# Twelve late row tiles: 32x32 turns on VectorE and transfers through DRAM in place of TensorE transposes

## The chip, the cores and the metric

The kernel runs on one core of a Trainium2 chip. Its time is the device time of the run in microseconds (us).

## What is computed

`x` is 4 batches of 512 rows of 512. Four stages each add a gated term to it. The change is about the hand-over into the third stage.

```python
x = x + tanh(g_xattn[0]) * L0_xattn(layernorm(x), ctx, ...)   # attention with one head of 128
x = x + tanh(g_ffn[0])   * L0_ffn(layernorm(x), ...)          # 512x512 product with bit planes
x = x + tanh(g_xattn[1]) * L1_xattn(layernorm(x), ctx, ...)   # 16 heads of 128, rms-normalised q and k
x = x + tanh(g_ffn[1])   * L1_ffn(layernorm(x), ...)          # 16 experts, the first batch's rows
# L1_xattn:
q, k = rmsnorm(h @ Wq, gq), rmsnorm(ctx @ Wk, gk)             # per head
out = softmax(q @ k.T / sqrt(128)) @ (ctx @ Wv)
return out @ Wo
```

## The kernel before

Each product is made of three matmuls on float32 values split in a high part (`_hi`) and the rest (`_lo`), so every operand is written twice: ScalarE mostly writes the high part, VectorE or GpSimd the rest.

The third stage runs as 64 items, `ITEMS`: first the 16 heads of batch 0, then for each head the batches 1, 2 and 3. It is a pipeline of steps `t`: in step `t` item `t` gets its keys, values and queries, item `u = t - 1` its scores and softmax, and item `w = t - 2` its product with the values and with `Wo`. Every engine has its own program, written out by hand in the function `step(t)` of that engine. Each runs its instructions in order, and semaphores tie them together. A step therefore starts on the engines at different times. Below, "step 10" means the instructions of `step(10)` on whatever engine.

Of SyncE the queue of transfers matters. In step `t` it issues, in this order and each behind its own wait: the key and value weights of the next head (`stage<-w`, buffer 0), the store of the probability pair (`turn<-prob`), the four loads that bring it back turned (`prob<-turn`), the query weights of the next head (`stage<-w`, buffer 1), and the output weights (buffer 2). The pair is two of the four 128x512 probability tiles of item `t - 1`. VectorE turns its 32x32 blocks in place (line 1580, `turn_quads`), and the store and loads put the blocks where they belong.

ScalarE begins `step(t)` by writing the high part of the turned pair (`moved_hi`). Then it copies the output weights (`split_wo`) and the query weights (`split_wq`) to their high parts, then the first key and value rows (`first_rows`, line 1071), and then comes the first exponential of the scores (`softmax(0)`, line 1032). `turn_quads` on VectorE waits for the second one, `softmax(1)`.

The projections of batches 1 to 3 need the layer-normalised `x` with its columns in the partitions (`xnT`). These twelve 128x512 row tiles are the late tiles: `LATE` gives one each to the steps 4 to 15. Batch 1 is first used in step 16. A tile in step `t` before the change:

- ScalarE, first thing in the step: `late_norm` (line 1185) writes the normalised rows to `xn`.
- TensorE, between two parts of the key and value products: `late_turn` (line 817), four 128x128 transposes into the bank `w_bank[1]`. It waits for `late_norm` and for VectorE to have emptied the bank.
- ScalarE: `late_copy` writes `xnT_hi` from the bank, between `first_rows` and `softmax(0)`.
- VectorE: `late_lower` writes `xnT_lo`, behind the two shifts that release `softmax(0)` and `softmax(1)`.
- TensorE waits for `late_lo` ahead of the second output product, since that one reuses the bank.

In the steps 4 to 15 all of this is one tile in each step of one head.

## Time and profile before

| | us |
|---|---|
| Median of 3 runs | 1406.72 (1406.38 to 1410.99) |
| The profiled execution's own time | 1406.11 |
| Its span | 1404.3 |
| TensorE matmul busy | 1376.5 |
| VectorE busy | 1140.6 |
| ScalarE busy | 976.5 |
| GpSimd busy | 942.4 |

The span is the time from the first to the last instruction of the trace. Positions ("at 307.20") are us from its start. A step's length is read as the distance between the same instruction of two steps on one engine. The names in a row are those of the program, output first, with buffer numbers left out.

### The profile page before, as it was taken

Reading aid. Unit: us, or ns where it says so; the run is one execution under the profiler, and the core shown is the slowest. Engines: PE = TensorE matmul, PEld = TensorE weight load, DVE = VectorE, ACT = ScalarE, POOL = GpSimd, SP = SyncE. Lnnn points to the kernel's source line nnn. Section 1 sums busy time; section 2 is a strip of 40 time slices with the busy share of each in tenths; the row PEclk is TensorE's granted clock in tenths of the full one; section 3 lists DMA queues with packets and bytes.
Section 4 is the critical chain, followed back from the end, with each engine's and each line's share of the span. In section 5 each row is a group of like instructions: output and inputs, shape, how many; then the busy total and the mean of one; then the engine's idle time right before and its main releaser. Section 6 shows DMA issues by size and latency. Waiting matters only on the chain.

```text
span 1404.3 us, 23125 instructions
## 1 busy us (share of the span) xinstructions
PE 1376.5 (98%) x7614; PEld 1175.1 (84%) x7614; DVE 1140.6 (81%) x2072; ACT 976.5 (70%) x2165; POOL 942.4 (67%) x729
## 2 busy tenths in 40 slices
PE   8899999999999999999999999999999999999998
PEld 6778778888888888888888888888888888877886
DVE  7888778788888888887878888887878787888777
ACT  7863467788876767667676767667676766666764
POOL 4876557777776567667676767676776757776561
PEclk9999999999999999999999999999999999999999
DMA  9420023333433555656564646566565653442312
GB/s 338 156 78 16 23 75 107 106 117 116 122 113 113 167 167 183 190 168 193 176 200 156 204 160 189 183 179 188 174 198 163 189 170 125 138 145 94 98 61 90
DMA packets 135734, 204.59 MB, mean 146 GB/s; under 512 B 10112, under 2 KB 70528, under 8 KB 135616
## 3 DMA queue, kind: packets, MB, share of 16 engines
q1 hardware_dynamic: 131856, 190.79, 42.7%
q0 software_dynamic: 3760, 12.32, 3.3%
q8 instruction: 62, 1.02, 0.3%
q14 instruction: 56, 0.46, 0.1%
HBM read 157.72 MB, written 45.35 MB: 145 GB/s over the span
## 4 chain that ended last, share of the span: by engine, by line
PE 76%; DVE 3%; POOL 2%; ACT 2%; DMA 1%; issue 1%; SPq 0%; ACTq 0%; POOLq 0%
PE j_bank L578 9%; PE j_bank L580 9%; PE j_bank L579 9%; PE w_bank L578 8%; PE w_bank L580 8%; PE w_bank L579 8%; PE s_bank L578 4%; PE s_bank L580 3%; PE s_bank L579 3%; PE t_bank L655 3%; PE t_bank L613 2%; PE t_bank L578 1%; PE t_bank L579 1%; PE t_bank L580 1%; PE w_bank L761 1%
## 5 line engine op out<-in xcount | busy, mean ns | idle before, releaser
L1032 ACT ACTIVATE prob<-s_bank,neg_bias,q_scale 128x512 f32<-128x512 f32 x255 | 197.4, 777 | 141.5 <-DVE neg_bias L1545 141.5
L1613 DVE SCALAR_TENSOR_TENSOR x_sb<-w_bank,inv_sum,x_sb 128x512 f32<-128x512 f32 x254 | 186.7, 745 | 32.0 <-PE w_bank L580 30.9
L1947 POOL TENSOR_TENSOR xnT_lo<-xnT_raw,xnT_hi 128x512 fp32r<-128x512 f32 (+2 forms) x47 | 126.4, 2691 | 63.1 <-ACT xnT_hi L990 63.1
L1524 DVE TENSOR_REDUCE neg_max<-s_bank 128x1 f32<-128x512 f32 x255 | 168.0, 679 | 0.9 <-PE s_bank L580 0.9
L578 PE MATMUL j_bank<-wkv_lo,cT_hi 128*128 128x256 f32 x512 | 145.0, 283 | 0.0
L1947 POOL TENSOR_TENSOR cT_round<-cT_raw,x_round 128x1408 fp32r<-128x1408 f32 (+1 forms) x31 | 104.4, 3367 | 59.9 <-ACT x_round L990 59.9
L580 PE MATMUL j_bank<-wkv_hi,cT_lo 128*128 128x256 f32 x512 | 144.4, 282 | 0.0
L579 PE MATMUL j_bank<-wkv_hi,cT_hi 128*128 128x256 f32 x512 | 144.2, 282 | 0.0
L1988 POOL TENSOR_TENSOR q_scale<-q_ss,minus_half 128x4 f32<-128x4 f32 x64 | 66.0, 1031 | 106.3 <-DVE q_ss L1537 106.3
L1947 POOL TENSOR_TENSOR sqs_lo<-xn,sqs_hi 128x512 fp32r<-128x512 f32 x62 | 104.0, 1677 | 34.5 <-ACT xn L1120 33.8
L1580 DVE STREAM_TRANSPOSE prob<-prob 128x1024 f32<-128x1024 f32 x59 | 73.5, 1245 | 60.8 <-ACT prob L1032 60.4
L1385 DVE TENSOR_TENSOR probT_lo<-t_bank,probT_hi 128x512 fp32r<-128x512 f32 x142 | 97.5, 687 | 23.1 <-ACT probT_hi L990 22.9
L1947 POOL TENSOR_TENSOR kv_lo<-kv_raw,kv_hi 128x512 fp32r<-128x512 f32 x68 | 89.1, 1311 | 37.0 <-DVE kv_hi L1594 35.7
L578 PE MATMUL w_bank<-wo_lo,oT_hi 128*128 128x512 f32 x254 | 107.9, 425 | 1.2 <-issue 1.0
L578 PE MATMUL s_bank<-kv_lo,qT_hi 128*128 128x512 f32 x255 | 106.6, 418 | 1.0 <-ACT prob L1032 0.5
L578 PE MATMUL j_bank<-xnT_lo,wq_hi 128*128 128x512 f32 x256 | 106.0, 414 | 1.0 <-POOL wq_lo L1947 1.0
L579 PEld LDWEIGHTS j_bank<-wkv_hi,cT_hi 128*128 128x128 f32 x512 | 97.2, 190 | 5.5
L578 PEld LDWEIGHTS j_bank<-wkv_lo,cT_hi 128*128 128x128 f32 x512 | 97.2, 190 | 5.2
L580 PE MATMUL j_bank<-xnT_hi,wq_lo 128*128 128x512 f32 x256 | 100.5, 392 | 0.0
L580 PE MATMUL s_bank<-kv_hi,qT_lo 128*128 128x512 f32 x255 | 100.2, 393 | 0.0
L580 PE MATMUL w_bank<-wo_hi,oT_lo 128*128 128x512 f32 x254 | 100.1, 394 | 0.0
L579 PE MATMUL j_bank<-xnT_hi,wq_hi 128*128 128x512 f32 x256 | 99.9, 390 | 0.0
(312 smaller groups left out, 4600.2 us busy)
## 6 DMA issues: line engine op xcount, KB each, us to landing
turn<-prob SPq DMA_DIRECT2D x59, 512.0 KB, 3.1
prob<-turn SPq DMA_DIRECT2D x236, 128.0 KB, 3.2
stage<-w SPq DMA_DIRECT2D x96, 256.0 KB, 3.5
xnT_raw<-w_gu SPq DMA_DIRECT2D x31, 704.0 KB, 4.5
cT_raw<-w_gu SPq DMA_DIRECT2D x31, 704.0 KB, 5.9
xnT_raw<-w_dn SPq DMA_DIRECT2D x16, 768.0 KB, 5.4
cT_raw<-w_dn SPq DMA_DIRECT2D x15, 768.0 KB, 5.4
planes<-bits SPq DMA_DIRECT2D x16, 512.0 KB, 5.0
```

The source lines that it names most:

```text
L578: pe.matmul(dst, lh, rl, start=first, stop=False)
L579: pe.matmul(dst, lh, rh, start=False, stop=False)
L580: return pe.matmul(dst, ll, rh, start=False, stop=last)
L613: last = pe.transpose(t_bank[0][:, j * P:(j + 1) * P], kv_raw[:, j, 0:HD], ident[:])
L655: last = pe.transpose(prob_bank(t, i)[:, j * P:(j + 1) * P], prob[:, i, j * P:(j + 1) * P], ident[:])
L1032: nc.scalar.activation(dst, src, ACT.Exp, bias=neg_bias[:, u % 2, i:i + 1], scale=q_scale[:, u % 2, i:i + 1], accum_out=row_sum[:, u % 2, ...
L1385: return nc.vector.tensor_tensor(dst, src, hi, ALU.subtract)
L1524: nc.vector.tensor_reduce(neg_max[:, u % 2, i:i + 1], score_bank(t, i)[:], AX_X, ALU.max, negate=True).then_inc(own_max, 1)
L1580: nc.vector.transpose(flat_pair, flat_pair).then_inc(p_quads, 1)
L1613: nc.vector.scalar_tensor_tensor(out=here, in0=w_bank[0][:] if packed else out_bank(t, i)[:], scalar=inv_sum[:, w % 2, i:i + 1], in1=here, ...
L1947: return nc.gpsimd.tensor_tensor(dst, src, hi, ALU.subtract)
L1988: nc.gpsimd.tensor_tensor(q_scale[:, u % 2, :], q_ss[:, u % 2, :], minus_half[:], ALU.pow).then_inc(q_scale_ready, 1)
```

## The change

A late tile is no longer turned by TensorE. In step `t`:

- ScalarE writes the normalised rows with the columns reordered in groups of 32 (`late_blocks`). It does so between `late_copy` and `softmax(0)` and no longer first in the step.
- VectorE turns the 32x32 blocks of the tile in place (`late_turn`, 128x512), in the place where `late_lower` was.
- SyncE stores the tile to a third plane of `turn` ahead of the pair's store, and reads it back with four loads behind the pair's loads, ahead of the query and output weights.
- In step `t + 1` ScalarE writes `xnT_hi` from `xn` (`late_copy(t - 1)`, in the old place), and GpSimd writes `xnT_lo` (`late_lower(t - 1)`) ahead of `scale_keys`.
- TensorE has neither the four transposes nor the wait for `late_lo` ahead of the second output product. It waits for the tiles of a batch once, at that batch's first query product (`LATE_NEEDED`).

```diff
--- before.py
+++ after.py
@@ -91,6 +91,7 @@
 TURN, TURNS = numbered("DFPR", L0_ORDER)
 LATE = {4 + n: key for n, key in enumerate((b, i) for b in range(1, B) for i in range(NT))}
 LATE_HEAD = min(LATE)
+LATE_NEEDED = {next(t for t, item in enumerate(ITEMS) if item[1] == b): NT * b for b in range(1, B)}
 XN, XNS = numbered("df", ACT_ORDER)
 MOMENTS, NMOMENTS = numbered("mCE", DVE_ORDER)
 SHIFT = {key: n for n, key in enumerate(key for key in POOL_ORDER if key[0] in "CE")}
@@ -311,7 +312,11 @@
         def late_tile(part, t):
 
             b, i = LATE[t]
-            return xnT[part][:, b, :, i * P:(i + 1) * P]
+            return xnT[part][:, b, :, i * P:(i + 1) * P].rearrange("p j (r c) -> p j r c", c=QUAD)
+
+        def late_blocks(t):
+
+            return late_row(t).rearrange("p (r j c) -> p j r c", j=DT, c=QUAD)
 
         def late_row(t):
 
...
@@ -493,7 +499,25 @@
                 sp.wait_ge(p_stored, 16 * (MOVES[u] + 1))
                 for c in range(NT):
                     sp.dma_start(prob[c * QUAD:(c + 1) * QUAD, 0:2, :].rearrange("a i (r m) -> a (i r) m", r=NT),
-                                 turn_dram.rearrange("i (r a) (c m) -> c a (i r) m", r=NT, c=NT)[c]).then_inc(p_moved, 16)
+                                 turn_dram[0:2].rearrange("i (r a) (c m) -> c a (i r) m", r=NT, c=NT)[c]).then_inc(p_moved, 16)
+
+            def store_late(t):
+
+                if t not in LATE:
+                    return
+                n = t - LATE_HEAD
+                sp.wait_ge(late_turned, n + 1)
+                wait(sp, late_moved, 16 * NT * n)
+                sp.dma_start(turn_dram[2], late_row(t)).then_inc(late_stored, 16)
+
+            def load_late(t):
+
+                if t not in LATE:
+                    return
+                sp.wait_ge(late_stored, 16 * (t - LATE_HEAD + 1))
+                for c in range(NT):
+                    sp.dma_start(late_row(t)[c * QUAD:(c + 1) * QUAD, :].rearrange("a (r m) -> a r m", r=NT),
+                                 turn_dram[2].rearrange("(r a) (c m) -> c a r m", r=NT, c=NT)[c]).then_inc(late_moved, 16)
 
             def expert(b):
                 return sp.value_load(block_expert[0:1, b:b + 1], min_val=0, max_val=E - 1)
@@ -539,8 +563,10 @@
                 if fresh(t):
                     key_weights(SET[t] + 1)
                 if not in_block(t):
+                    store_late(t)
                     store_pair(t - 1)
                     load_pair(t - 1)
+                    load_late(t)
                 if fresh(t):
                     query_weights(SET[t] + 1)
                 if fresh(t - 2):
@@ -682,8 +708,6 @@
                         return
                     if t == LAST_VALUES and i == 2:
                         need(pe, o_lo, 1, w, 2)
-                    if t in LATE and i == 1:
-                        pe.wait_ge(late_lo, t - LATE_HEAD + 1)
                     if i == 0:
                         if not packed:
                             need(pe, o_lo, 1, w, 1)
@@ -727,6 +751,8 @@
                     if 0 in tiles:
                         if fresh(t):
                             pe.wait_ge(wq_lo, SET[t] + 1)
+                        if t in LATE_NEEDED:
+                            pe.wait_ge(late_lo, LATE_NEEDED[t])
                         need(pe, kv_first, 1, t, 1)
                     for dj in tiles:
                         last = product(j_bank[1][:], [a[:, dj * HD:(dj + 1) * HD] for a in wq],
@@ -807,15 +833,6 @@
                                 last = product(w_bank[0][:, to:to + width], here,
                                                [a[:, half, at:at + width] for a in (hi, lo)], j == 0, j == IT - 1)
                     last.then_inc(d_mm, 1)
-
-                def late_turn():
-                    if t not in LATE:
-                        return
-                    pe.wait_ge(late_normed, t - LATE_HEAD + 1)
-                    need(pe, w_added, 4, w, 0)
-                    for j in range(DT):
-                        last = pe.transpose(w_bank[1][:, j * P:(j + 1) * P], late_row(t)[:, j * P:(j + 1) * P], ident[:])
-                    last.then_inc(late_turned, 1)
 
                 def key_values():
                     key_value(0)
@@ -870,7 +887,6 @@
                     key_value(0, (0,))
                     query_squares()
                     key_value(0, (1,))
-                    late_turn()
                     key_value(1)
                     values()
                     if t == 2:
@@ -1181,15 +1197,16 @@
                     b, i = LATE[t]
                     act.wait_ge(shift_ready, SHIFT["E", b] + 1)
                     act.wait_ge(blocks_ready, 1)
-                    wait(act, late_turned, t - LATE_HEAD - 1)
-                    nc.scalar.activation(late_row(t), x_sb[:, b, i, :], ACT.Identity, bias=ln_shift[:, b, i:i + 1],
+                    wait(act, late_lo, t - LATE_HEAD - 1)
+                    row = x_sb[:, b, i, :].rearrange("p (j r c) -> p j r c", j=DT, c=QUAD)
+                    nc.scalar.activation(late_blocks(t), row, ACT.Identity, bias=ln_shift[:, b, i:i + 1],
                                          scale=rstd[:, b, i:i + 1]).then_inc(late_normed, 1)
 
-                def late_copy():
-                    if t not in LATE:
-                        return
-                    act.wait_ge(late_turned, t - LATE_HEAD + 1)
-                    copy_hi(late_tile(0, t), w_bank[1][:].rearrange("p (j q) -> p j q", j=4)).then_inc(late_hi, 1)
+                def late_copy(v):
+                    if v not in LATE:
+                        return
+                    act.wait_ge(late_moved, 16 * NT * (v - LATE_HEAD + 1))
+                    copy_hi(late_tile(0, v), late_blocks(v)).then_inc(late_hi, 1)
 
                 if t == 0:
                     return key_parts, query_parts, query_squares, key_hi
@@ -1229,7 +1246,6 @@
                     if t + 1 < NI and fresh(t + 1):
                         split_wkv(t + 1)
 
-                late_norm()
                 if not in_block(t - 1):
                     moved_hi(w)
                 if packed:
@@ -1265,7 +1281,8 @@
                 if fresh(t):
                     split_wq(t)
                 first_rows()
-                late_copy()
+                late_copy(t - 1)
+                late_norm()
                 softmax(0)
                 softmax(1)
                 second_rows()
@@ -1693,12 +1710,11 @@
                     need(dve, q_squared, 2, t, 2)
                     lower(sqs[1][:], squares(t), f32(sqs[0][:])).then_inc(sq_lo, 1)
 
-                def late_lower():
+                def late_turn():
                     if t not in LATE:
                         return
-                    dve.wait_ge(late_hi, t - LATE_HEAD + 1)
-                    lower(late_tile(1, t), w_bank[1][:].rearrange("p (j q) -> p j q", j=4),
-                          f32(late_tile(0, t))).then_inc(late_lo, 1)
+                    dve.wait_ge(late_normed, t - LATE_HEAD + 1)
+                    nc.vector.transpose(late_row(t), late_row(t)).then_inc(late_turned, 1)
 
                 def key_values_lo():
                     key_lo()
@@ -1799,7 +1815,7 @@
                     block_experts()
                 shift(0)
                 shift(1)
-                late_lower()
+                late_turn()
                 if t == T0 - 2:
                     dve.wait_ge(w_added, 4 * (LAST[0] + 1))
                     statistics(0, 0, NMOMENTS)
@@ -2054,6 +2070,12 @@
                     need(pool, q_squared, 2, t, 2)
                     lower(sqs[1][:], squares(t), f32(sqs[0][:])).then_inc(sq_lo, 1)
 
+                def late_lower(v):
+                    if v not in LATE:
+                        return
+                    pool.wait_ge(late_hi, v - LATE_HEAD + 1)
+                    lower(late_tile(1, v), late_blocks(v), f32(late_tile(0, v))).then_inc(late_lo, 1)
+
                 if t == 0:
                     return scale_keys, squares_lo, values_lo
                 if up:
@@ -2070,6 +2092,7 @@
                 if t > 2 and fresh(t):
                     lower_wq(t)
                 gate_up_lo()
+                late_lower(t - 1)
                 scale_keys()
                 take_y(2)
                 values_lo()
...
```

SyncE's queue in one step with a late tile, before. The names are tile and tensor, output first, and the waits are the semaphores on which the row waits. The three `stage<-w1` rows are the key and value weights (waits `wkv_lo`), the query weights (`wq_lo`) and the output weights (`wo_lo`):

```order
L466 DMA stage<-w1 128x512 [waits wkv_lo]
L487 DMA turn<-prob 128x2x512 [waits p_moved,p_quads]
L495 DMA prob<-turn 32x8x128 [waits p_stored]
L495 DMA prob<-turn 32x8x128 x3
L466 DMA stage<-w1 128x512 [waits wq_lo]
L466 DMA stage<-w1 128x512 [waits wo_lo]
```

The same place of the queue in the changed kernel:

```order
L472 DMA stage<-w1 128x512 [waits wkv_lo]
L511 DMA turn<-xn 128x512 [waits late_moved,late_turned]
L493 DMA turn<-prob 128x2x512 [waits p_moved,p_quads]
L501 DMA prob<-turn 32x8x128 [waits p_stored]
L501 DMA prob<-turn 32x8x128 x3
L519 DMA xn<-turn 32x4x128 [waits late_stored]
L519 DMA xn<-turn 32x4x128 x3
L472 DMA stage<-w1 128x512 [waits wq_lo]
L472 DMA stage<-w1 128x512 [waits wo_lo]
```

The tile's store stands ahead of the pair's store, and its four loads (32 partitions of four pieces of 128 elements each) stand between the pair's loads and the query and output weights.

ScalarE at the start of a step with a late tile, from the layer norm to the two exponentials that the pair's turn waits for, before (`xn<-x_sb` is `late_norm`, `xnT_hi` is `late_copy`):

```order
L1185 ACTIVATE xn<-x_sb,ln_shift,rstd 128x512 [waits late_turned,blocks_ready,shift_ready]
L990 CAST probT_hi<-prob 128x8x4x32 [waits pv_mm,p_moved]
L990 CAST wo_hi<-stage 128x512 [waits w_mm,wo_in]
L990 CAST wq_hi<-stage 128x512 [waits q_mm,wq_in]
L1071 COPY kv_raw<-j_bank1 128x512 [waits v_lo,kT_mm,kv_mm]
L990 CAST xnT_hi<-w_bank1 128x4x128 [waits late_turned]
L1032 ACTIVATE prob,row_sum<-s_bank0,neg_bias,q_scale 128x4x4x32 [waits pair_lo,s_max]
```

ScalarE at the same place in the changed kernel:

```order
L1006 CAST probT_hi<-prob 128x8x4x32 [waits pv_mm,p_moved]
L1006 CAST wo_hi<-stage 128x512 [waits w_mm,wo_in]
L1006 CAST wq_hi<-stage 128x512 [waits q_mm,wq_in]
L1087 COPY kv_raw<-j_bank1 128x512 [waits v_lo,kT_mm,kv_mm]
L1006 CAST xnT_hi<-xn 128x4x128 [waits late_moved]
L1202 ACTIVATE xn<-x_sb,ln_shift,rstd 128x4x4x32 [waits late_lo,blocks_ready,shift_ready]
L1048 ACTIVATE prob,row_sum<-s_bank0,neg_bias,q_scale 128x4x4x32 [waits pair_lo,s_max]
```

The layer norm moved from the front of the step to a place behind the weights' copies and `late_copy`, directly ahead of the two exponentials, and `late_copy` now waits for the transfers (`late_moved`).

## Rows read from the trace of the kernel before

**Rows 1.** The page's heading and its busy times, share of the span in brackets.

```profile
span 1404.3 us, 23125 instructions
PE 1376.5 (98%) x7614; PEld 1175.1 (84%) x7614; DVE 1140.6 (81%) x2072; ACT 976.5 (70%) x2165; POOL 942.4 (67%) x729
```

**Rows 2.** Busy time by stretch: twelve steps with a late tile, then two without.

```profile
core 0: us, PE busy (x) PEld busy (x) DVE busy (x) ACT busy (x) POOL busy (x), PEclk, DMA share, GB/s
205.00:392.00 187.00, 187.00 (x1050) 159.79 (x1049) 150.68 (x281) 150.17 (x355) 139.60 (x116) 1.00 0.38 116
404.00:435.00 31.00, 31.00 (x171) 26.27 (x170) 24.02 (x46) 22.35 (x56) 19.89 (x18) 1.00 0.30 95
```

**Rows 3.** Timeline (start us, us, engine, line): first matmul of the query squares, once a step.

```profile
210.13 0.39 PE L742 MATMUL t_bank<-sqs_hi,ones 128*128 128x512 f32 x1
226.28 0.39 PE L742 MATMUL t_bank<-sqs_hi,ones 128*128 128x512 f32 x1
...
403.84 0.40 PE L742 MATMUL t_bank<-sqs_hi,ones 128*128 128x512 f32 x1
419.54 0.39 PE L742 MATMUL t_bank<-sqs_hi,ones 128*128 128x512 f32 x1
435.24 0.39 PE L742 MATMUL t_bank<-sqs_hi,ones 128*128 128x512 f32 x1
```

**Rows 4.** Line 817, all TensorE turns of the late tiles: ns min/median/max, first and last start.

```profile
L817 PE MATMUL w_bank<-ident,xn x48: 270/272/276, 211.3 to 389.2; 128*128 128x128 f32 x48
```

**Rows 5.** Timeline of SyncE's queue: pair stores of steps 4, 9, 15, 16, and what follows.

```profile
217.13 0.38 SPq L487 DMA_DIRECT2D turn<-prob  x1
...
297.86 0.38 SPq L487 DMA_DIRECT2D turn<-prob  x1
300.65 1.81 SPq L495 DMA_DIRECT2D prob<-turn  x4
302.50 2.48 SPq L466 DMA_DIRECT2D stage<-w  x3
...
394.70 0.38 SPq L487 DMA_DIRECT2D turn<-prob  x1
...
410.70 0.38 SPq L487 DMA_DIRECT2D turn<-prob  x1
...
415.35 0.92 SPq L466 DMA_DIRECT2D stage<-w  x2
```

**Rows 6.** Waits of SyncE's queue, 205 to 392 us: total, times, longest.

```profile
SPq L495 <- DMA turn<-prob: 28.6, 11, 3.0
```

**Rows 7.** Weight loads of steps 4 to 15: durations, and time to landing.

```profile
L466 SPq DMA_DIRECT2D stage<-w x36: 327/430/786, 206.3 to 385.4; - x36
DMA to landing us min/median/max: 2.8/3.4/4.1
```

**Rows 8.** Timeline of ScalarE, step 10; the first row is of step 4.

```profile
210.88 0.62 ACT L990 CAST wo_hi<-stage 128x512 fp32r<-128x512 f32 x1 [0.44 <-DMA stage<-w]
...
305.54 0.84 ACT L1185 ACTIVATE xn<-x_sb,ln_shift,rstd 128x512 f32<-128x512 f32 x1
306.26 1.06 ACT L990 CAST probT_hi<-prob 128x1024 fp32r<-128x1024 f32 x1
307.20 0.63 ACT L990 CAST wo_hi<-stage 128x512 fp32r<-128x512 f32 x1
307.72 0.64 ACT L990 CAST wq_hi<-stage 128x512 fp32r<-128x512 f32 x1
308.37 0.59 ACT L1071 COPY kv_raw<-j_bank 128x512 f32<-128x512 f32 x1
308.85 0.60 ACT L990 CAST xnT_hi<-w_bank 128x512 fp32r<-128x512 f32 x1
311.07 0.78 ACT L1032 ACTIVATE prob<-s_bank,neg_bias,q_scale 128x512 f32<-128x512 f32 x1 [1.62 <-DVE neg_bias L1545]
```

**Rows 9.** Line 1580 on VectorE, 205 to 392 us: busy, mean ns, idle before.

```profile
L1580 DVE STREAM_TRANSPOSE prob<-prob 128x1024 f32<-128x1024 f32 x11 | 13.7, 1246 | 10.8 <-ACT prob L1032 10.8
```

**Rows 10.** Timeline of GpSimd, step 10.

```profile
312.00 1.30 POOL L1947 TENSOR_TENSOR wq_lo<-stage,wq_hi 128x512 fp32r<-128x512 f32 x1
314.91 0.20 POOL L2036 TENSOR_TENSOR k_ms<-k_ss,eps 128x4 f32<-128x4 f32 x1 [1.61 <-ACT xn L1096]
```

**Rows 11.** Timeline of step 16, without a late tile: ScalarE's exponentials 0 and 2, TensorE's turn.

```profile
407.77 0.78 ACT L1032 ACTIVATE prob<-s_bank,neg_bias,q_scale 128x512 f32<-128x512 f32 x1 [1.97 <-DVE neg_bias L1545]
412.13 0.78 ACT L1032 ACTIVATE prob<-s_bank,neg_bias,q_scale 128x512 f32<-128x512 f32 x1 [0.60 <-DVE neg_bias L1545]
413.28 0.60 PE L655 MATMUL t_bank<-ident,prob 128*128 128x128 f32 x4
```

More of the change, by code:

```diff
@@ L375, in flamingo_kernel @@
             sem("p_quads"), sem("p_stored"), sem("p_moved"), sem("pair_hi"), sem("pair_lo"))
-        late_normed, late_turned, late_hi, late_lo = (
-            sem("late_normed"), sem("late_turned"), sem("late_hi"), sem("late_lo"))
+        late_normed, late_turned, late_stored, late_moved, late_hi, late_lo = (
+            sem("late_normed"), sem("late_turned"), sem("late_stored"), sem("late_moved"), sem("late_hi"),
+            sem("late_lo"))
         pv_mm, o_hi, o_lo, w_mm, w_added = sem("pv_mm"), sem("o_hi"), sem("o_lo"), sem("w_mm"), sem("w_added")
@@ L486, in store_pair @@
                 wait(sp, p_moved, 16 * NT * MOVES[u])
-                sp.dma_start(turn_dram.rearrange("i p m -> p i m"), prob_pair).then_inc(p_stored, 16)
+                sp.dma_start(turn_dram[0:2].rearrange("i p m -> p i m"), prob_pair).then_inc(p_stored, 16)
             def load_pair(u):
@@ L2209 @@
     x0 = nc.dram_tensor("x0", (S, D), F32, kind="Internal").ap()
-    turn = nc.dram_tensor("turn", (2, P, S), F32, kind="Internal").ap()
+    turn = nc.dram_tensor("turn", (3, P, S), F32, kind="Internal").ap()
     flamingo_kernel(nc, *args, x0, rows, y, turn, out)
```

## The prediction

> **What bounds the kernel now.** The page's head comes first: TensorE's matmuls are busy 1376.5 of 1404.3 us [rows 1], but a busy share is only an average, so the stretch of the change is looked at by itself. From 205 to 392 us, the steps with a late tile, TensorE's matmuls are busy 187.00 of 187.00 us at a granted clock of 1.00, which is the 2.4 GHz level. VectorE, ScalarE and GpSimd are at 81, 80 and 75% [rows 2]. So TensorE is the bound there and every other engine has some room.
>
> The second view is one instruction that TensorE runs once a step. From step 4 to step 16 the query squares move from 210.13 to 403.84 us, 16.14 us a step. The two steps after that have no late tile and take 15.70 us [rows 3]. The reader is to see that this difference of 0.44 us is what a late tile costs today, all else equal. Twelve tiles make 5.3 us. No more than that can be won here, since TensorE is busy all the time in the two plain steps as well [rows 2].
>
> **What is removed.** Forty-eight transposes of 272 ns each [rows 4]. They overlap, so their durations don't add up to the gain. The gain is the 0.44 us of the step lengths. The wait for `late_lo` costs nothing today, since TensorE isn't idle.
>
> **What is added, engine by engine.**
>
> VectorE: a 128x512 turn in place of a 128x512 subtraction. The pair's 128x1024 turn takes 1246 ns [rows 9], so half of it, 0.62 us, is an estimate for the tile, within a tenth of a us of what goes. It stands where the subtraction stood, ahead of a wait of 10.8 us over 11 times for ScalarE [rows 9], about 1 us a step. Counted as nothing. If that cover went, VectorE would pay 0.62 us a step.
>
> GpSimd: one more 128x512 subtraction, 1.30 us like `wq_lo` [rows 10]. It goes between `wq_lo` and `k_ms`, where GpSimd idles 1.61 us for ScalarE [rows 10]. Covered with 0.3 us to spare. Without this cover the turned keys would be late by what sticks out.
>
> ScalarE: `late_copy` from SBUF and not from PSUM, about 0.52 us between starts (`wo_hi` to `wq_hi`), and `late_norm`, 0.72 us to the next start [rows 8]. Their number is the same, but the layer norm leaves the front of the step and stands directly ahead of `softmax(0)`. Today ScalarE idles 1.62 us there [rows 8], so it fits, as long as the copies of the weights start on time.
>
> SyncE: this is where I expect the gain to go. The tile's store is issued before the pair's and is under way while VectorE turns the pair, so I count it as nothing. But the tile's four loads are ahead of the query and output weights in a queue that runs in order. The pair's four loads take 1.85 us to issue, from 300.65 to 302.50 [rows 5]. They are twice as large as the tile's. The weight loads, 256 KB each, take 0.46 us each (two in 0.92) [rows 5], which is the same spacing at another size, so the spacing doesn't follow the bytes and the tile's four loads cost 1.85 us too. Both weight loads of the next head are late by that much. Their readers, `split_wo` and `split_wq`, stand ahead of `softmax(0)` on ScalarE, and `turn_quads` waits for `softmax(1)` and is what the next pair store waits for. That closes a loop through the queue, from one pair store to the next:
>
> - pair store to first pair load: 0.38 of issue and 28.6 / 11 = 2.60 of waiting [rows 5, 6], 2.98
> - pair's loads 1.85, tile's loads 1.85 (new), query weights 0.46 [rows 5]
> - output weights, issue to landing: 3.4, the median of the 36 weight loads [rows 7]
> - ScalarE from `wo_hi` to `softmax(0)`: 0.52 + 0.52 + 0.48 for the weights and rows, 0.52 for `late_copy`, 0.72 for `late_norm` (new in this place) [rows 8], 2.76
> - `softmax(0)` to the pair store, 407.77 to 410.70 in step 16 [rows 5, 11], 2.93
>
> The sum is 16.23 us, against 15.70 of TensorE. Today's loop checks the reading: the first parts give a landing of the output weights at 297.86 + 8.69 = 306.55, and `wo_hi` starts at 307.20, when ScalarE has finished the layer norm and the pair [rows 5, 8]. So the loop has slack today, and only step 4 shows a wait for the weights (0.44 us) [rows 8].
>
> **The sum.** The late loads of steps 4 to 15 lengthen twelve intervals between pair stores, 217.13 to 410.70, 193.57 us today [rows 5]. In their place stand 12 x 16.23 = 194.8. Step 16 has no layer norm, which gives 0.72 back. TensorE is not disturbed until the loop has eaten its lead: in a step of 15.70 us it begins the turn of tile 2 at 413.28, and the exponential that it needs ended at 412.13 + 0.78 = 412.91 [rows 11]; of these 0.37 us some 0.1 is the hand-over (an estimate), which leaves 0.27. Change: 194.8 - 0.72 - 0.27 - 193.57 = +0.2 us. The profiled execution took 1406.11 us, 1.8 more than its span, and would take 1406.3. The median of the runs is 0.6 above that execution, so I say 1407.
>
> The open number is the landing time. Each tenth of a us is worth 1.2 us. Its bounds are 2.8 and 4.1 us [rows 7]. At 2.8 the loop takes 15.63, TensorE is the bound and all 5.3 us are won. At 4.1 it takes 16.93, and the change is +8.6 us. I take the median. The output weights would find a queue that carries less for each us of issue (64 KB per load of the tile), but there is also more in flight.
>
> The Trainium skill speaks against my middle value ("DMA: Bandwidth & Descriptors", the section on the anatomy of one DMA): a transfer takes about 2.0 us plus its bytes at 436 GB/s, measured on GpSimd's path. By it the 256 KB would land after 2.6 us, as an estimate, and the loop would take 15.4 us, so that the full gain would stand. No weight load in this stretch was that quick (least 2.8) [rows 7], so I give it no more than the rival below already has.
>
> **The rivals.**
>
> *The full gain.* TensorE stays the bound, each step takes 15.70, and the run ends at 1406.11 - 5.3 + 0.6 = 1401.4. For it: TensorE is busy all the time, and each other engine has its cover. Against it: it needs a loop under 15.7 us, a landing below 2.9. A gain of over 4.2 us needs a landing of 3.0 or a piece of the chain that I have counted twice. 25%.
>
> *The queue costs more than it spares: slower.* The place is the output weights' copy on ScalarE, the price is 1.2 us for each tenth of a us of landing, and it decides from a landing of 3.7 us (a loop of 16.6). The tile adds 512 KB of traffic a step to the 38% busy DMA engines [rows 2], and one load of weights has taken 4.1 us already [rows 7]. At 4.0 us the run would take 1414. 22%.
>
> *GpSimd becomes late.* If its added subtraction ends after the key squares, the turned keys are late. Its spare time is 0.3 us; if it sticks out by as much as it takes to cost 0.4 us a step, the loop's time grows to 16.6 and the run to 1411. GpSimd's place in the chain is behind that of the weights, so a late ScalarE gives it time. 3%.
>
> **How the numbers follow.** The likeliest case, the loop near 16.2 us, has 50%, and its time is 1407, with its own range of 1403 to 1411. The full gain has 25% and the two slower rivals together 25%. The range of 1400.5 to 1413 takes in the full gain and a landing of up to 3.9 us, and leaves out some 2 in 10. A measurement of this kernel tells about 0.3%, 4.2 us, from no change. Faster by more than that has 0.25, within it 0.50, slower 0.25.
>
> **What would show it.** In the changed kernel's timeline the query squares of steps 5 to 16 would be some 16.2 us apart, and TensorE would have idle time that ends with ScalarE's exponentials. ScalarE's `wo_hi` would wait for DMA in nearly every step, where it waited once. The queue would show eight loads in a row of about 3.7 us. VectorE's and GpSimd's added instructions would have no one waiting for them. The prediction is wrong if the steps are 15.70 long (the landing is quicker, or the weights are not what `softmax(0)` waits for), or if `moved_hi` or the turned keys show up as a new wait.

## The result, and the profile after

The changed kernel is slower: 1413.98 us median (1411.58 to 1416.73, 16 runs), against 1408.78 us (1406.38 to 1412.83, 16 runs) of the kernel before in the same session. The ratio is 1.0035 with a 95% interval of 1.0025 to 1.0045, some 5 us. The prediction said 1407.0, 1400.5 to 1413.0, and no change as the likeliest case. The kernel before had a median of 1406.72 in the three runs known then, so 2.1 us of the 7 us miss is the level of the runs. The other 4.9 us lie in the change itself, 5.2 us against the 0.3 of the forecast.

The page of the changed kernel, heading and first busy row:

```profile
span 1412.2 us, 23090 instructions
PE 1378.5 (98%) x7566; PEld 1169.6 (83%) x7566; DVE 1140.9 (81%) x2072; ACT 975.3 (69%) x2165; POOL 958.0 (68%) x741
```

The busy times hardly differ from [rows 1]. The stretch of the late tiles does. Busy time by stretch:

```profile
core 0: us, PE busy (x) PEld busy (x) DVE busy (x) ACT busy (x) POOL busy (x), PEclk, DMA share, GB/s
205.00:400.00 195.00, 189.79 (x1020) 155.60 (x1018) 153.30 (x285) 151.99 (x360) 156.62 (x130) 1.00 0.45 143
```

TensorE, busy all of the time in [rows 2], now idles 5.2 of 195 us at the same clock. That understates the loss, since the ends of matmuls are modelled in the profile: the step lengths below show more. Who waits for whom in that stretch (total us, times, longest us):

```profile
ACT wo_hi L1006 <- DMA stage<-w: 28.3, 12, 3.6
PEld s_bank L604 <- ACT prob L1048: 9.3, 16, 1.8
DVE prob L1597 <- ACT prob L1048: 9.0, 11, 1.0
PE s_bank L604 <- ACT prob L1048: 4.3, 5, 1.4
PEld t_bank L681 <- ACT prob L1048: 3.4, 11, 0.4
```

The reader is to see two rows. ScalarE's copy of the output weights waits for its transfer in all twelve steps, 28.3 us in total, where it waited once for 0.44 us [rows 8]. And TensorE's scores wait for ScalarE's exponentials (`s_bank <- ACT prob`), which they did in none of these steps before. The query squares show what that does to the steps:

```profile
212.53 0.39 PE L768 MATMUL t_bank<-sqs_hi,ones 128*128 128x512 f32 x1
228.23 0.40 PE L768 MATMUL t_bank<-sqs_hi,ones 128*128 128x512 f32 x1
245.80 0.39 PE L768 MATMUL t_bank<-sqs_hi,ones 128*128 128x512 f32 x1
...
311.90 0.39 PE L768 MATMUL t_bank<-sqs_hi,ones 128*128 128x512 f32 x1
327.72 0.39 PE L768 MATMUL t_bank<-sqs_hi,ones 128*128 128x512 f32 x1
...
426.46 0.39 PE L768 MATMUL t_bank<-sqs_hi,ones 128*128 128x512 f32 x1
442.18 0.39 PE L768 MATMUL t_bank<-sqs_hi,ones 128*128 128x512 f32 x1
```

Step 4 to step 5 takes 15.70, which is TensorE's pace without a late turn. Then come 17.57, ... 15.82, and so on: from 228.23 to 426.46 twelve steps take 198.23 us, 16.52 each, in place of 16.14 [rows 3], and 9.8 us more than twelve of 15.70. Behind them a step takes 15.72 again. Step 4 itself is 2.40 us later in this profile than before (212.53 against 210.13 [rows 3]). That lies ahead of the change, so the two spans differ by more than the medians do (7.9 us against 5.2). Here is one of the slow steps over the queue, ScalarE, VectorE and TensorE, by timeline (rows left out):

```profile
219.40 0.38 SPq L493 DMA_DIRECT2D turn<-prob  x1
222.35 1.80 SPq L501 DMA_DIRECT2D prob<-turn  x4
224.20 1.87 SPq L519 DMA_DIRECT2D xn<-turn  x4
226.12 1.38 SPq L472 DMA_DIRECT2D stage<-w  x3
226.77 1.07 ACT L1006 CAST probT_hi<-prob 128x1024 fp32r<-128x1024 f32 x1
231.45 0.62 ACT L1006 CAST wo_hi<-stage 128x512 fp32r<-128x512 f32 x1 [3.62 <-DMA stage<-w]
232.98 0.62 ACT L1006 CAST xnT_hi<-xn 128x512 fp32r<-128x512 f32 x1
233.50 0.81 ACT L1202 ACTIVATE xn<-x_sb,ln_shift,rstd 128x512 f32<-128x512 f32 x1
234.21 0.76 ACT L1048 ACTIVATE prob<-s_bank,neg_bias,q_scale 128x512 f32<-128x512 f32 x1
234.34 0.71 DVE L1717 STREAM_TRANSPOSE xn<-xn 128x512 f32<-128x512 f32 x1 [2.09 <-ACT xn L1202]
234.97 0.77 ACT L1048 ACTIVATE prob<-s_bank,neg_bias,q_scale 128x512 f32<-128x512 f32 x1
235.08 0.33 SPq L511 DMA_DIRECT2D turn<-xn  x1
235.12 0.50 PE L604 MATMUL s_bank<-kv_lo,qT_hi 128*128 128x512 f32 x1 [1.37 <-ACT prob L1048]
237.13 0.38 SPq L493 DMA_DIRECT2D turn<-prob  x1
```

Every link that the prediction named is there. The pair's store is issued at 219.40 and its four loads at 222.35. The tile's four loads take the queue until 226.12, and only then are the weights issued. The output weights are the second of the three. These take 1.38 us together and 0.43 each, so their starts are 0.47 us apart, and the output weights are issued at 226.59. ScalarE has the turned pair done at 227.84 and then waits 3.62 us. Behind `wo_hi` the weights, the rows, `late_copy` and `late_norm` run without a gap until the exponential at 234.21. TensorE's scores waited 1.37 us for it and start at 235.12, and the next pair store is issued at 237.13, 17.73 us after the last.

### The profile page after: what moved, and what is told of

Same layout as the page of the kernel before. It is cut to its first block, busy times and chain, and to the rows that moved or that the text cites. A ratio compares the mean times of both kernels' runs of the same rounds, so it can differ in the third digit from the quotient of the medians.

```text
span 1412.2 us, 23090 instructions
## 1 busy us (share of the span) xinstructions
PE 1378.5 (98%) x7566; PEld 1169.6 (83%) x7566; DVE 1140.9 (81%) x2072; ACT 975.3 (69%) x2165; POOL 958.0 (68%) x741
## 4 chain that ended last, share of the span: by engine, by line
PE 63%; DVE 3%; POOL 2%; ACT 1%; issue 1%; DMA 1%; SPq 0%; ACTq 0%; POOLq 0%
PE j_bank L604 8%; PE j_bank L606 8%; PE j_bank L605 8%; PE w_bank L604 7%; PE w_bank L606 7%; PE w_bank L605 7%; PE s_bank L604 3%; PE s_bank L606 3%; PE s_bank L605 3%; PE t_bank L681 3%; PE t_bank L639 1%; PE w_bank L787 1%; PE t_bank L604 1%; PE w_bank L815 1%; PE t_bank L605 1%
```

## The experiments

Below, an interval is the time from one pair's store to the next, and "landing" is the start of `wo_hi` less the start of the output weights' issue, where ScalarE waited for them. The profile of the changed kernel has no landing time of its own for these loads. Each kernel here runs against the kernel before of its own session.

**The tile's loads behind the weights** (`tile_loads_behind`).

```diff
                     load_pair(t - 1)
-                    load_late(t)
                 if fresh(t):
                     query_weights(SET[t] + 1)
                 if fresh(t - 2):
                     out_weights(SET[t - 2] + 1)
+                load_late(t)
```

> The changed kernel with the tile's four loads issued behind the query and output weights and not ahead of them. Queue theory (the weights are issued 1.85 us late, and their copies on ScalarE stand ahead of the exponentials): the loop from pair store to pair store loses 1.85 us and is under TensorE's 15.70 again, the steps with a late tile take 15.70, and the run is 5.3 us faster than the kernel before (ratio 0.996), 10 us faster than the change. Rival, the added work: the turn on VectorE, the subtraction on GpSimd or the layer norm ahead of softmax(0) cost the time; then the order of the loads changes nothing and the run stays 4 to 5 us slower than before.

1404.23 us median of 12 runs, ratio to before 0.9973 (0.9964 to 0.9982). Nine of the twelve intervals from pair store to pair store are 15.68 to 15.71 long, the other three 15.87, 15.92 and 15.98 (later expectations say four). That is why the ratio is a little above the 0.996 that I expected. Its stretch, and its wait for the output weights:

```profile
205.00:400.00 195.00, 194.79 (x1068) 165.16 (x1067) 160.15 (x298) 162.31 (x381) 162.88 (x135) 1.00 0.49 152
```

```profile
ACT wo_hi L1006 <- DMA stage<-w: 7.5, 11, 1.2
```

TensorE is busy 194.79 of 195 us, and the wait for the weights has fallen from 28.3 to 7.5 us. All the added instructions of VectorE, ScalarE and GpSimd are still there. So the added work costs nothing here, and the place of four loads in a queue is the difference between 0.9973 and 1.0035.

**The tile in one load, and with a quarter of its bytes** (`tile_in_one_load`, `tile_quarter_bytes`). These two separate the number of issues from the bytes. Both leave out part of the transposition, so they serve for timing only.

```diff
-                for c in range(NT):
-                    sp.dma_start(late_row(t)[c * QUAD:(c + 1) * QUAD, :]...,
-                                 turn_dram[2]...[c]).then_inc(late_moved, 16)
+                sp.dma_start(late_row(t), turn_dram[2]).then_inc(late_moved, 16)
```

> The changed kernel with one load of the whole 256 KB tile in the place of the four of 64 KB. The blocks are read back as they were stored and not put in their places, so this leaves out part of the transposition. Issue theory: three issues of 0.46 us less, 1.4 us a step, the bytes are the same: nearly the full gain, 3 to 5 us faster than before (0.997). Traffic theory (what the weights wait for is the tile's 256 KB on the DMA engines): the same bytes are in front of the weights, and the run stays 4 to 5 us slower than before (1.0035).

```diff
                 for c in range(NT):
-                    sp.dma_start(late_row(t)[c * QUAD:(c + 1) * QUAD, :]...,
-                                 turn_dram[2]...[c]).then_inc(late_moved, 16)
+                    sp.dma_start(late_row(t)[c * QUAD:(c + 1) * QUAD, 0:P]...,
+                                 turn_dram[2]...[c][:, 0:1]).then_inc(late_moved, 16)
```

> The changed kernel with the tile's four loads in their place, but each with a quarter of its bytes (128 of 512 columns), so part of the transposition is left out. Issue theory: the weights are issued as late as in the change, and the run stays 4 to 5 us slower than before (1.0035), with weights that land at most 0.2 us sooner. Traffic theory: 192 KB less a step ahead of the weights at some 250 GB/s are 0.8 us a step, the run is 4 us or more faster than the change and no slower than before.

One load of the same 256 KB: 0.9979 (0.9969 to 0.9989). Four loads with a quarter of the bytes: 1.0020 (1.0010 to 1.0029). The twelve intervals add up to 188.6 us in the first and 196.7 us in the second, against 198.2 in the changed kernel. Three issues are worth 9.6 us, even cut off as they are by TensorE's 15.70 a step. Three quarters of the bytes are worth 1.5. The single load also has longer pieces, but `tile_quarter_bytes` has a quarter of the short pieces and is nearly as slow as the change, so the pieces are not it. The issues make the change slow, and the bytes have a small part.

**The layer norm back in front** (`norm_in_front`), and **with the loads behind as well** (`norm_front_loads_behind`).

```diff
+                late_norm()
                 if not in_block(t - 1):
                     moved_hi(w)
 ...
                 late_copy(t - 1)
-                late_norm()
```

> The changed kernel with the layer norm of the tile back at the front of ScalarE's step. Queue theory with the loop: the loop loses 0.72 us a step, since ScalarE then does the layer norm while it waits for the output weights, but a step can't get under 15.70; taken step by step from the changed kernel's trace that is 6 us less than the change, about 1 us faster than the kernel before (ratio 0.999). Rival (the weights' lateness is not in a loop, each step pays its own stall of TensorE at the scores): the layer norm's place matters just once, and the run stays within 1 us of the change (1.0035).

1.0000 (0.9989 to 1.0011). This supports the loop: the place of one 0.72 us instruction on ScalarE moved the run by 5 us. But one thing did not fit. Ten of the twelve intervals were within 16.05 and 16.18, and where the loop was short they did not go down to 15.70. Something other than the queue held them, and it was not TensorE, which idled 1.8 of 195 us. The second kernel was made to find out.

> The changed kernel with both reversals: the tile's loads behind the weights and the layer norm at the front of ScalarE's step. TensorE has no late turn and the weights are on time. Second-wall theory (with the layer norm in front of the copy of the turned pair, GpSimd's subtraction of the pair ends 0.4 us after TensorE could start the values' product): the steps stay at about 16.08, as with the layer norm in front alone, and the run within 1.5 us of the kernel before (0.999 to 1.0005). Rival (the queue was what held norm_in_front at 16.08): the steps take 15.70 and the run is 4 to 5 us faster than before (0.997).

1.0004 (0.9994 to 1.0013), with eleven of twelve intervals 16.08 to 16.11, though the weights are early again and no layer norm stands behind them. Here is the reason, in the timeline of GpSimd, ScalarE and TensorE (rows left out), and below it the same place in the kernel before:

```profile
308.31 0.84 ACT L1202 ACTIVATE xn<-x_sb,ln_shift,rstd 128x512 f32<-128x512 f32 x1
309.03 1.05 ACT L1006 CAST probT_hi<-prob 128x1024 fp32r<-128x1024 f32 x1
310.16 2.42 POOL L1963 TENSOR_TENSOR probT_lo<-prob,probT_hi 128x1024 fp32r<-128x1024 f32 x1 [0.82 <-ACT probT_hi L1006]
310.51 0.62 ACT L1006 CAST wo_hi<-stage 128x512 fp32r<-128x512 f32 x1 [0.43 <-DMA stage<-w]
312.27 0.28 PE L606 MATMUL j_bank<-wkv_hi,cT_lo 128*128 128x256 f32 x1
312.67 0.47 PE L604 MATMUL t_bank<-probT_lo,kv_hi 128*128 128x512 f32 x1
```

```profile
307.39 2.41 POOL L1947 TENSOR_TENSOR probT_lo<-prob,probT_hi 128x1024 fp32r<-128x1024 f32 x1 [0.83 <-ACT probT_hi L990]
310.04 0.40 PE L578 MATMUL t_bank<-probT_lo,kv_hi 128*128 128x512 f32 x1
```

The layer norm at the front delays the copy of the turned pair (`probT_hi<-prob`), which ends at 310.08. GpSimd's subtraction (`probT_lo`) starts on it at 310.16 and ends at 312.58, and the values' product on TensorE starts at 312.67, 0.40 us behind the matmul ahead of it, where these matmuls are otherwise 0.12 apart. It is so in eleven of the twelve steps of both kernels: 0.10 us from the end of the subtraction to the product. In the kernel before the product starts 0.24 us behind the end of the subtraction (309.80 to 310.04), so only 0.14 us were to spare. So there are two walls close together. TensorE's 0.44 us for the late turn mostly filled a gap that the turned pair would have made anyway: without the turn the steps went from 16.14 to 16.08. Taking the turn off TensorE gains next to nothing until the layer norm leaves the front. I did not run the other half, the layer norm moved alone with the turn left on TensorE.

**The loads alone, in the kernel before** (`before_with_four_loads`).

```diff
+            def spare_loads(t):
+                if t not in LATE:
+                    return
+                for c in range(NT):
+                    sp.dma_start(stage[c * QUAD:(c + 1) * QUAD, 3, :]..., x[0:P, :]...[c]).then_inc(spare_in, 16)
 ...
                     load_pair(t - 1)
+                    spare_loads(t)
                 if fresh(t):
                     query_weights(SET[t] + 1)
```

> The kernel before, with four loads of 64 KB from x into an idle plane that nobody reads, in the place where the change has the tile's loads. TensorE still turns the tiles and the layer norm stays at the front. Loop theory: without the layer norm ahead of softmax(0) the loop is about 15.8 us in a mean step, under the 16.14 us of this kernel; only steps in which the output weights land over 4 us after their issue pass it, four of twelve by 0.2 to 0.9 us: 1 to 2 us slower than before (ratio 1.001). Rival (the loads by themselves are the cost of the change): 5 us slower (1.0035) or, since TensorE's 0.44 us a step are still there, 10 us slower (1.007).

0.9999 (0.9991 to 1.0008). Queue and ScalarE in one of its steps:

```profile
289.81 2.10 SPq L504 DMA_DIRECT2D stage<-x  x4
291.96 1.38 SPq L467 DMA_DIRECT2D stage<-w  x3
297.18 0.62 ACT L1000 CAST wo_hi<-stage 128x512 fp32r<-128x512 f32 x1 [2.53 <-DMA stage<-w]
```

The weights are as late as in the changed kernel, and ScalarE waits for them, but the layer norm isn't between them and the exponentials. Nine of the intervals are 16.12 to 16.19, one is 16.95 (the step shown), the one behind it is 15.67 and takes half of that back, and the last is 16.00. Only one step passed TensorE's pace, where I expected four, so the 1 to 2 us that I expected did not come. The four loads cost nothing by themselves, and they cost time only where the loop is closed and longer than everything else.

**One load more** (`five_loads`).

```diff
+                sp.dma_start(stage[0:QUAD, 3, :]..., turn_dram[2]...[0]).then_inc(spare_in, 16)
```

> The changed kernel with a fifth load of 64 KB behind the tile's four, into an idle plane that nobody reads. Loop theory: each issue ahead of the weights adds 0.46 us to each of twelve intervals, so 5.5 us more than the change, a ratio to before of 1.0075. Rival (a stall that is paid once, or a queue with slack left): 1.5 us or less more than the change, under 1.005.

1.0061 (1.0048 to 1.0074) in 5 runs, below the 1.0075 that I expected and above the rival's 1.005. Its wait for the output weights:

```profile
ACT wo_hi L1009 <- DMA stage<-w: 32.0, 12, 3.7
```

Twelve intervals take 201.9 us, 3.7 more than the changed kernel. The query weights are issued 0.50 us later in the mean (7.21 after the pair's store, against 6.71), and `wo_hi` starts 0.32 us later (11.21 against 10.89). The missing third is not spread over the steps. In the eight steps with a short landing in the changed kernel `wo_hi` starts 0.48 us later, so the issue is paid whole. In the four with a long one it starts no later in the mean, since their landing is shorter here (3.7 to 4.5 us in place of 4.3 to 4.9). What is special about these four comes with `key_weights_held`.

**The weights in the store's wait** (`weights_in_store_wait`).

```diff
                     store_pair(t - 1)
-                    load_pair(t - 1)
-                    load_late(t)
                 if fresh(t):
                     query_weights(SET[t] + 1)
                 if fresh(t - 2):
                     out_weights(SET[t - 2] + 1)
+                if not in_block(t):
+                    load_pair(t - 1)
+                    load_late(t)
```

> The changed kernel with the query and output weights issued right behind the pair's store, in the 2.6 us in which the queue waits for that store, and the pair's and the tile's loads behind them. With the tile's loads behind the weights four steps of twelve were still 15.86 to 15.98 long, where the output weights landed over 4.2 us after their issue. Queue theory: the weights get 1.8 us more, all steps take 15.70, about 1 us faster than with the tile's loads behind (ratio to before 0.9966). Rival, contention: 512 KB of weights are on the DMA engines together with the pair's store and ahead of the pair's loads; the store or the loads get 0.5 us or more slower, the turned pair is late for GpSimd's subtraction and the values' product, and the run is no faster than with the tile's loads behind (0.9973 or above).

0.9988 (0.9978 to 0.9997), worse than with the tile's loads behind by the medians' ratios, though the two intervals overlap. The twelve intervals bear it out, 190.4 us against 189.0. ScalarE never waits for the weights any more, but:

```profile
ACT probT_hi L1007 <- DMA prob<-turn: 4.0, 7, 1.0
POOL probT_lo L1964 <- ACT probT_hi L1007: 5.6, 7, 1.2
```

`moved_hi` waits for the pair's loads seven times. Their first issue is mostly 3.1 us behind the store and not 2.8, and they share the DMA engines with the weights. The pair is the other thing that is due early in a step, so what is put ahead of it is paid there. The rival of that run was right.

**The key weights held back** (`key_weights_held`). The landing of the output weights was longer than predicted, and I suspected the key weights, which now follow them without a gap.

```diff
-                if fresh(t):
+                if fresh(t) and t not in LATE:
                     key_weights(SET[t] + 1)
                 if not in_block(t):
                     store_late(t)
+                    if t in LATE:
+                        key_weights(SET[t] + 1)
```

> The changed kernel with the next key weights issued behind the tile's store of the following step, and not right behind the output weights. Now the three weight loads are issued 0.43 us apart, where before the third came 1.3 us later. Theory, sharing: the output weights land later in part because the key weights are on the DMA engines with them; without them the landing gets 0.2 to 0.3 us shorter, the run 2.4 to 3.6 us faster than the change (ratio to before 1.0015). Rival (the long landings come from something else on one DMA engine, the packets of instructions): the run stays within 1.2 us of the change (1.003 or above) and the long landings of 4.4 to 4.9 us stay.

1.0035 (1.0022 to 1.0048) in 5 runs, the same as the change.

```profile
ACT wo_hi L1008 <- DMA stage<-w: 27.5, 12, 3.6
```

The sharing theory fell: the mean landing is 3.66 us, against 3.70 in the changed kernel. The four long landings (4.3 to 4.9 us) are in the same four steps of ScalarE as in the changed kernel (5, 8, 12 and 15). What those have in common shows in the transfers. First the step of the timeline above, from 225.9 to 231.9 us (each character or number of the first two rows is 0.15 us: the share of the 16 DMA engines that is busy, and GB/s):

```profile
DMA  6920693899828799989988988622010000000000
GB/s 147 236 65 14 143 260 109 263 154 109 164 96 218 273 396 341 301 273 451 355 328 314 369 341 328 232 82 68 27 27 14 14 27 27 27 14 27 27 0 0
q8 instruction: 1, 0.02, 1.3%
stage<-w SPq DMA_DIRECT2D x3, 256.0 KB, 3.1
```

Then a step with a short landing, in the same two views, from 309.68 to 315.68 us, and the issue and the read of its weights:

```profile
DMA  8547266297738999999889986410000000000000
GB/s 263 140 137 219 79 181 198 48 143 137 82 137 300 369 410 396 382 341 355 314 301 341 382 341 246 164 68 14 0 0 0 0 0 0 0 0 0 0 0 0
stage<-w SPq DMA_DIRECT2D x3, 256.0 KB, 2.8
```

```profile
309.76 1.38 SPq L472 DMA_DIRECT2D stage<-w  x3
313.36 0.62 ACT L1006 CAST wo_hi<-stage 128x512 fp32r<-128x512 f32 x1 [1.85 <-DMA stage<-w]
```

In the second, the traffic ends at once and the output weights are read 3.1 us after their issue (309.76 + 0.47 to 313.36). In the first, it falls to 14 to 27 GB/s and stays there for some 1.5 us, and `wo_hi` starts near its end. The semaphore's updates in the trace say what that is: a load raises it 16 times. In all twelve steps 15 of them have come 2.9 to 3.3 us after the issue. The last comes within 3.5 us in eight steps and at 4.3 to 4.8 us in the four slow ones, and `wo_hi` starts 0.02 us behind it. So one part of sixteen is late. In the slow window there is one packet of the queue q8, instructions. It has 16 KB and takes 1.29 us, where most 2 KB packets of the weights take 0.08.

In the changed kernel, `tile_quarter_bytes` and `key_weights_held` together, ScalarE waited for the output weights in all 36 intervals. The 12 with a landing of 4.33 us or more all have such a packet that starts 1.7 to 2.3 us behind the issue. The 24 others, 2.81 to 3.88 us, have none before the read. The long step of `before_with_four_loads` (4.75) has one too, 1.9 us behind the issue. Where the packet falls seems to matter as well. In `five_loads` it starts 0.5 to 0.7 us behind the issue in three of the four steps, and these landings are 3.7, 4.3 and 4.5. In `norm_in_front` it starts 2.8 to 3.0 us behind in three steps, and these are 3.2 to 3.5. But there are also long landings without a packet in kernels with another order of the transfers: 4.1 to 4.5 us in four steps of `tile_in_one_load`, 4.2 and 4.4 in `tile_loads_behind`, up to 4.8 in `norm_front_loads_behind`. In the last two the tile's loads are in flight behind the weights. And one load of key weights in the kernel before landed after 2.8 us with such a packet 2.1 us behind its issue. I did not change the instruction stream to move the packets, so this is a correlation and not an experiment. The 3.1 us in the view of the slow step is no landing of the output weights: of the three loads of that row only the first, the query weights, has a landing in this profile.

**The output weights first** (`out_weights_first`), the loads behind and the two weight loads in the order in which ScalarE reads them.

```diff
                     load_pair(t - 1)
-                if fresh(t):
-                    query_weights(SET[t] + 1)
                 if fresh(t - 2):
                     out_weights(SET[t - 2] + 1)
+                if fresh(t):
+                    query_weights(SET[t] + 1)
+                load_late(t)
```

> The changed kernel with the tile's loads behind the weights and the output weights issued before the query weights, in the order in which ScalarE reads them. Queue theory: the output weights land 0.46 us sooner, so the four steps of 15.86 to 15.98 that were left get 15.70 to 15.75, 0.7 us less in all: 0.9968 or so, hardly to be told from 0.9973. Rival (the query weights, now the later ones, take over): their copy starts 0.52 us behind that of the output weights, so a landing 0.46 us later than today's costs nothing; if it did, the run would be 0.5 to 1 us slower than with the tile's loads behind.

0.9962 (0.9949 to 0.9975) in 5 runs, 1403.15 us against 1408.75 of the kernel before, the fastest of all. Its waits for the two weights:

```profile
ACT wq_hi L1006 <- DMA stage<-w: 3.0, 6, 1.4
ACT wo_hi L1006 <- DMA stage<-w: 0.3, 1, 0.3
```

ScalarE's wait for the output weights is down to 0.3 us in total, and it now waits 3.0 us for the query weights, for which it never waited with the tile's loads behind. That costs nothing: ten of twelve intervals are 15.69 to 15.72, the step with the 1.4 us among them. From `tile_loads_behind` its interval doesn't separate it. Both beat both given kernels.

## Why the prediction was wrong

The step that failed is a term of the sum: "output weights, issue to landing: 3.4, the median of the 36 weight loads". It measured 3.70 us in the mean. The mechanism was right and this size was off. Means over the twelve intervals of the changed kernel (for `wo_hi` to `softmax(0)` over the eleven with a layer norm):

| part of the loop | predicted | measured |
|---|---|---|
| pair store to first pair load | 2.98 | 2.90 |
| first pair load to the query weights (eight loads) | 3.70 | 3.81 |
| query weights to output weights | 0.46 | 0.47 |
| output weights, issue to read | 3.4 | 3.70 |
| `wo_hi` to `softmax(0)` | 2.76 | 2.76 |
| `softmax(0)` to the pair store | 2.93 | 2.92 |
| sum, a step with a layer norm | 16.23 | 16.56 |

The sum had 194.8 - 0.72 - 0.27 = 193.8 us for the twelve intervals, and they took 198.24, so 4.5 us are missing. The landing is 3.6 of them. The eight loads gave 1.4 more and the pair store's part 0.9 less. The 0.27 us of TensorE's lead that the sum took off doesn't show in these intervals, and the small terms make up the rest.

Why was 3.4 too short? Not because a median was taken of [rows 7]: the mean of the same 36 loads is 3.41. Two other things are in it. The 36 are three kinds of load, and the twelve loads of output weights among them took 3.58 us in the mean. With that the loop would have been 16.41 and the run 2 us slower than I said. And the changed kernel has four landings of 4.3 to 4.9 us, longer than any in [rows 7]. Its eight others average 3.25, and its median is 3.42. So the number held as a median, and the loop pays the mean. Why these four are so long was not shown beyond the correlation with the packets, and the rows of the kernel before could not have given them. The range's upper end allowed a landing of 3.9 at the price of 1.2 us for each tenth, but on the lower level of the three runs shown. The measured median passed it by 1.0 us, less than the 2.1 us between the levels.

Point by point:

- TensorE's part was right in size and incomplete. Steps of 15.70 and a gain of 5.4 us by the ratio were there for `out_weights_first` (0.9962). But I said that the 0.44 us was the turn's alone. `norm_front_loads_behind` shows that without the turn the turned pair holds the steps at 16.08, and that moving the layer norm, which I counted as a cost, is also what makes the gain possible.
- VectorE's turn took 0.71 us and not 0.62, and nothing but its own store waited for it. GpSimd was never late: its wait for the key squares was still there (14.9 us in the stretch). The rival of a late GpSimd had no part.
- The queue and the loop were right, link by link, and so was the reading that the cost of an issue doesn't follow the bytes (`tile_in_one_load`, `tile_quarter_bytes`).
- "The queue costs more than it spares", with 22%, was the case that came. It was said to decide from a landing of 3.7 us, and the landing was 3.70, just at its edge.
- The estimate by the Trainium skill ("DMA: Bandwidth & Descriptors", anatomy of one DMA), 2.6 us for 256 KB, is too short for these loads: in the changed kernel no read of the output weights came less than 2.94 us after their issue, and the mean was 3.70. The page's figure is of GpSimd's path, and these loads are SyncE's, with others in flight.

## What to carry to other kernels

A transfer has a place in its queue, and its cost is what stands behind it: look up who reads each later transfer, and follow that reader until it leads back to the queue. Once a loop is closed, it pays each issue, each instruction moved into it and the mean (not the median) of each latency. Take a latency from the rows of that very transfer, and leave room for a tail that the kernel before doesn't show. Where an engine is busy all the time, check also what would stop it next, since a second wait may lie right behind the work that is taken away.

## What the runs showed of the hardware that was not expected

A landing of a 256 KB load has two sizes in three of these kernels: 2.81 to 3.88 us, and 4.3 to 4.9 us in each of the 12 steps in which a 16 KB packet of instructions started 1.7 to 2.3 us behind the issue. Of the 16 updates by which the load's semaphore tells of its landing, 15 are on time in the changed kernel and the last is 1.3 to 1.6 us late. Meanwhile the traffic falls to 14 to 27 GB/s. The long ones were in the same steps of all three kernels, so they belong to the schedule and not to chance. Whether the packet is the cause stays open.
